# One block for eight stages: the barriers between the stages of a layer chain give way to waits on data

## The reference

```python
x = x + _L0_xattn_ref(_layernorm(x), ctx, ctx, Wq, Wk, Wv, Wo)    # 32 heads of 16, grouped keys
x = x + _L0_ffn_ref(_layernorm(x), c1_w, c2_w, w1, w2t)           # one hidden unit of each block of 32
x = x + _L1_xattn_ref(_layernorm(x), ctx, Wq, Wk, Wv, Wo)         # 16 heads of 96 over ctx and x
x = x + _L1_ffn_ref(_layernorm(x), W, b, lora_A, lora_B)          # Hadamard rotation, W, low-rank part
x = x + _L2_xattn_ref(_layernorm(x), ctx, mask, Wq, Wk, Wv, Wo, q_norm_w, k_norm_w)  # 32 heads of 128
x = x + _L2_ffn_ref(_layernorm(x), weight)                        # operands rounded to fp8 by a global scale
x = x + _L3_xattn_ref(_layernorm(x), ctx, ctx)                    # correlation by Fourier transforms, top 9 lags
x = x + _L3_ffn_ref(_layernorm(x), w1, s1, w2, s2, w3, s3)        # gated unit, weights of 4 bits
```

## Time and profile before

| | |
|---|---|
| times of 3 runs | 1519.96, 1521.7, 1523.2 us; median 1521.7 |
| span of the profiled execution | 1519.0 us (the runs take 1 to 4 us more than this span) |
| PE busy | 1394.3 us, 92% of the span |
| DVE, ACT, POOL busy | 1080.1, 762.1, 718.3 us |
| stages 0 to 7 end at | 171.5, 351.7, 651.2, 684.0, 1204.1, 1246.9, 1339.0, 1519.0 us |
| PE's pause at the seven crossings | 4.26, 6.02, 3.57, 5.16, 3.97, 4.74, 3.68 us; sum 31.4 |

### The profile page before, as it was taken

One profiled execution on the slowest core, in us unless ns is written; L12 is line 12 of the kernel. 1 busy time (PEld: TensorE's weight loads), 2 busy tenths in 40 slices (PEclk: granted clock), 3 DMA queues, 4 the chain that ended last, 5 costly groups with the idle time before them and its releaser, 6 DMA issues. The chain is left out here.

```text
span 1519.0 us, 31488 instructions
## 1 busy us (share of the span) xinstructions
PE 1394.3 (92%) x11352; PEld 830.9 (55%) x11352; DVE 1080.1 (71%) x2125; ACT 762.1 (50%) x2476; POOL 718.3 (47%) x748
## 2 busy tenths in 40 slices
PE   5798599997999999887999999999999788889998
PEld 4676244445777777444655555555555335434444
DVE  7997665645666666667989888898877779966212
ACT  4777363222434432347666666666665457655111
POOL 4888551001433434845666666665665306734000
PEclk9999799999999999999999999999999898989999
DMA  7999572215999988766775655655545401546000
GB/s 189 186 174 181 124 171 42 35 35 122 174 195 184 170 142 136 127 144 147 154 150 112 113 115 111 140 109 115 105 79 79 123 3 32 127 84 112 17 12 28
DMA packets 524570, 174.63 MB, mean 115 GB/s; under 512 B 482576, under 2 KB 507600, under 8 KB 524416
## 3 DMA queue, kind: packets, MB, share of 16 engines
q1 hardware_dynamic: 524416, 172.62, 59.0%
HBM read 53.27 MB, written 2.10 MB: 36 GB/s over the span
## 5 line engine op out<-in xcount | busy, mean ns | idle before, releaser
L1946 POOL TENSOR_TENSOR a_q_ss<-a_q_ss,half 128x4 f32<-128x4 f32 x64 | 90.1, 1408 | 167.6 <-DVE a_q_ss L1855 84.0
L67 PE MATMUL bank<-a_wq_hi,xn_pair 128*128 128x512 f16 (+1 forms) x384 | 140.8, 367 | 10.9 <-DVE a_kn L1860 5.2
L1768 ACT ACTIVATE a_probs<-a_masked,a_negmax 128x128 f32<-128x128 f32 x256 | 99.6, 390 | 101.6 <-DVE a_negmax L1826 101.6
L1285 POOL TENSOR_TENSOR a_p_hl<-a_probs,a_p_hl 128x512 f16<-128x512 f32 x64 | 74.3, 1162 | 142.3 <-DVE a_p_hl L1209 142.3
L68 PE MATMUL bank<-a_wq_lo,xn_pair 128*128 128x512 f16 (+1 forms) x384 | 140.5, 366 | 0.0
L69 PE MATMUL bank<-a_wq_hi,xn_pair 128*128 128x512 f16 (+1 forms) x384 | 140.3, 365 | 0.0
L67 PE MATMUL bank<-a_wo_hi,a_o_hi 128*128 128x512 f16 x256 | 97.8, 382 | 4.4 <-DVE x_state L1842 3.5
L68 PE MATMUL bank<-a_wo_lo,a_o_hi 128*128 128x512 f16 x256 | 97.7, 382 | 0.0
L69 PE MATMUL bank<-a_wo_hi,a_o_lo 128*128 128x512 f16 x256 | 97.5, 381 | 0.0
L1961 POOL TENSOR_TENSOR a_normal<-a_probs,a_recip 128x512 f32<-128x512 f32 x64 | 90.2, 1410 | 5.0
L716 POOL TENSOR_TENSOR a_p_hl<-a_probs,a_p_hl 128x512 f16<-128x512 f32 x64 | 78.0, 1230 | 23.6 <-DVE a_p_hl L627 16.7
(11 more groups left out here) (467 smaller groups left out, 5022.4 us busy)
## 6 DMA issues: line engine op xcount, KB each, us to landing
a_no<-in_L_xattn_Wo SPq DMA_DIRECT2D x9, 1024.0 KB, 5.7
a_nq<-in_L_xattn_Wq SPq DMA_DIRECT2D x8, 1024.0 KB, 5.8
a_n_wq<-in_L_xattn_Wq SPq DMA_DIRECT2D x4, 768.0 KB, 5.7
a_n_wo<-in_L_xattn_Wo SPq DMA_DIRECT2D x4, 768.0 KB, 6.1
a_nk<-in_L_xattn_Wk SPq DMA_DIRECT2D x9, 256.0 KB, 3.0
a_nv<-in_L_xattn_Wv SPq DMA_DIRECT2D x9, 256.0 KB, 3.1
f_v_hat<-in_L_ffn_w SPq DMA_DIRECT2D x2, 1152.0 KB, 6.2
x_state<-in_x SPq DMA_DIRECT2D x8, 256.0 KB, 5.2
```

The lines of the kernel that those rows point to most:

```text
L67: pe.matmul(out, lh, rh, start=start, stop=False)
L1285: pool.tensor_tensor(p_hl[s % PN][:, 1, t, :], probs[unit(s, t) % PROBS][:, :, :].rearrange("p h n -> p (h n)"), p_hl[s % PN][:, 0, t, :], ...
L1768: m = act.activation(probs[s % 2][:, h, :], src, ACT.Exp, bias=negmax[s % 2][:, h:h + 1], accum_out=total[s % 2][:, h:h + 1])
L1946: pool.tensor_tensor(r[:, :], r[:, :], K.half[:, 0:n], ALU.pow).then_inc(root_done.sem, 1)
```

## The change

All stages are put into one block, made once in `build`; each stage appends to the five programs of that block, so an engine goes on from its last instruction of a stage to its first of the next. `end_stage` emits nothing any more. What the barrier gave is replaced as follows.

- A bank counts as free at the start: `n_free` and `n_drained` go down by one, `wait_free` leaves out the wait of a first use, and the loops of `pe.sem_inc` are gone.
- Each engine ends a stage (but the last) with `K.leave`: a drain that raises the engine's own `left` semaphore.
- The clearing of the last stage's semaphores moves into the next stage, on POOL: `clear_last_stage` waits until all five engines have left the last stage. It stands at a step of POOL's program: stage 1 at step `NT`, stage 2 at step 4, stage 3 after the root of the last row and the bias additions, stage 4 at step 2, stage 5 after the root of the last row, stage 6 at step 3. Stage 7 clears nothing.
- SP waits at the start of stages 2 and 6 until PE has left the stage before (`K.enter(sp, "pe")`), because it loads into memory that PE read.
- Two data waits are new: in stage 3 PE waits for each piece of `f_w_lo` (`merged_lo`, raised by L1273), and in stage 6 PE's first two queries wait for DVE's rows (`first_rows`, raised by L2870).

```diff
     def n_free(self, use, turn=0):
-        return turn * self.per[self.slot[use]] + self.nth[use] + 1
+        return turn * self.per[self.slot[use]] + self.nth[use]
+
+    def wait_free(self, pe, use, turn=0):
+        if self.n_free(use, turn):
+            pe.wait_ge(self.freed(use), self.n_free(use, turn))
...
     def n_drained(self, use, turn=0):
-        return turn * self.per[self.slot[use]] + self.nth[use] + 2
+        return turn * self.per[self.slot[use]] + self.nth[use] + 1
...
-        self.in_use = []
+        self.in_use, self.of_last, self.stage = [], [], 0
+        self.left = {e: nc.alloc_semaphore(name=f"left_{e}") for e in ("sp", "pe", "act", "dve", "pool")}
...
+    def enter(self, engine, *others):
+        for e in others:
+            engine.wait_ge(self.left[e], self.stage)
+
+    def leave(self, engine, name):
+        engine.drain().then_inc(self.left[name], 1)
+
+    def clear_last_stage(self):
+        self.enter(self.nc.gpsimd, *self.left)
+        self.nc.clear_and_free_semaphores(self.of_last)
+
     def end_stage(self):
-        self.nc.clear_and_free_semaphores(self.in_use)
-        self.nc.all_engine_barrier()
-        self.in_use = []
+        self.of_last, self.in_use = self.in_use, []
+        self.stage += 1
...
-        with nc.Block() as block:
-            @block.sync
-            def _(sp):
+        @K.block.sync
+        def _(sp):
+            K.enter(sp, "pe")
...
+            K.leave(sp, "sp")
...
-            @block.tensor
-            def _(pe):
-                for banks in (s_bank, o_bank, ring, y_bank):
-                    for freed in banks.freed_sems:
-                        pe.sem_inc(freed, 1)
...
+                if f < AHEAD[1][0]:
+                    pe.wait_ge(S.first_rows.sem, S.first_rows.count(f))
...
 def build(nc, a, out):
     with ExitStack() as ctx:
         K = Kernel(nc, ctx)
+        K.block = ctx.enter_context(nc.Block())
```

More of the change, by code:

```diff
@@ L99, in take_stats @@
         return dve.bn_stats(self.stats[:, at, :], self.x[:, at, :])
-    def end_stage(self):
-        self.nc.clear_and_free_semaphores(self.in_use)
-        self.nc.all_engine_barrier()
-        self.in_use = []
[L108 to L147, removed]
-            pe.sem_inc(freed, 1)
[L149 to L171, removed]
@@ new lines, in _, with turn @@
+        @K.block.sync
+        def _(sp):
+            def turn(b, src, here):
+                sp.dma_start_transpose(K.xn_pair[:, :, :, b * P:(b + 1) * P].rearrange("p a k n -> p (a k) n"),
+                                       src[:, :, :].rearrange("p a n -> p (a n)")).then_inc(here, 16)
+            for kind in ("wk", "wq", "wv"):
+                first.load(sp, kind, 0, first.w_in[kind])
+            first.load_columns(sp)
+            sp.wait_ge(last_lo_done, 1)
+            turn(LAST, last_hl, last_in)
+            first.load(sp, "wo", 0, first.w_in["wo"])
+            for b in ahead:
+                sp.wait_ge(next_lo.sem, next_lo.count(b))
+                sp.wait_ge(y_bank.filled(b), y_bank.n_filled(b))
+                turn(b, xn_hl[b % XB], next_in[b % XB])
+            sp.wait_ge(last_in, 16)
+            K.leave(sp, "sp")
@@ new lines, in _ @@
+        @K.block.tensor
+        def _(pe):
+            for b in batches:
+                if b == LAST:
+                    pe.wait_ge(last_in, 16)
+                else:
+                    pe.wait_ge(rot.next_in[b % rot.XB], 16 * (b // rot.XB + 1))
+                y_bank.wait_free(pe, b)
+                for k in range(KT):
+                    if b == 0:
+                        pe.wait_ge(rot.merged_lo.sem, rot.merged_lo.count(k))
+                    m = pair_matmul(pe, y_bank[b][:, :], tuple(t[:, k, b * P:(b + 1) * P] for t in (K.xn_hi, K.xn_lo)),
+                                    rot.merged(k), k == 0, k == KT - 1)
+                m.then_inc(y_bank.filled(b), 1)
+            for i, use in enumerate(first.MADE):
+                first.make(pe, use, K.bank[i])
+            K.leave(pe, "pe")
@@ new lines, in _ @@
+        @K.block.scalar
+        def _(act):
+            act.wait_ge(last_xn_done, 1)
+            act.activation(last_hl[:, 0, :], last_xn[:, :], ACT.Copy).then_inc(last_hi_done, 1)
+            for t in steps:
+                for b in ready(t, 1):
+                    act.wait_ge(next_root.sem, next_root.count(b))
+                    if b >= XN:
+                        act.wait_ge(next_lo.sem, next_lo.count(b - XN))
+                        act.wait_ge(next_in[b % XB], 16 * (b // XB))
+                    act.activation(xn[b % XN][:, :], K.x[:, b, :], ACT.Identity, bias=nxt.shift[:, b:b + 1],
+                                   scale=nxt.rstd[:, b:b + 1]).then_inc(next_xn.sem, 1)
+                    act.wait_ge(next_xn.sem, next_xn.count(b))
+                    act.activation(xn_hl[b % XB][:, 0, :], xn[b % XN][:, :], ACT.Copy).then_inc(next_hi.sem, 1)
+                for use in split_at(t):
+                    first.high(act, use)
+            K.leave(act, "act")
@@ L2951, in __init__ @@
         self.tab = K.sem("x3_tab")
+        self.first_rows = Steps(K.nc.alloc_semaphore(name="x3_first_rows"), [0, 1])
     def load(self, sp):
```

4419 lines of the change are left out of this document (2137 added, 2282 removed).

## The result

The changed kernel takes 1505.16 us (median of 4 runs, 1504.09 to 1505.43) against 1520.83 us before (median of 4, 1517.4 to 1523.2). The ratio is 0.9896, with a 95% interval of 0.988 to 0.9912: 1.0% faster, 15.7 us. The profiled spans are 1503.1 us and 1519.0 us.

A forecast was written before the change was run, and what follows sets the result against it. PE was taken to bound the kernel, its 31.4 us of crossing pauses being the ceiling. The terms 0 + 2.7 + 2.9 + 2.6 + 2.0 + 2.5 + 1.1 = 13.8 us off 1521.7 gave 1508, range 1500 to 1514.5.

The forecast's parts named there:

- What bounds the kernel: PE, busy 92% of the span, ends the kernel; its seven crossing pauses, together 31.4 us, cap the direct gain.
- 0 to 1: 0: Stage 0 to 1: PE's pause goes, but ACT's split still waits for a landing, so 0 us gained.
- 1 to 2: -2.7: Stage 1 to 2: SP's loads go out sooner and the load behind a_wo_hi lands sooner, 2.7 us gained.
- 2 to 3: -2.9: Stage 2 to 3: PE goes on with a wait per piece and DVE's queue starts sooner, 2.9 us gained.
- 3 to 4: -2.6: Stage 3 to 4: block end, barrier and eleven PE increments go before ACT's squares of the keys, 2.6 us gained.
- 5 to 6: -2.5: Stage 5 to 6: PE starts just behind DVE's first row, with first_rows raised row by row, 2.5 us gained.
- 6 to 7: -1.1: Stage 6 to 7: PE still waits for the last transposing transfer's landing, so only 1.1 us gained.
- 4 to 5: -2.0: Stage 4 to 5: DVE's aggregate and PE's transpose, said to read DVE's last reduction, come sooner, 2.0 us gained.
- What is added: Seven drains per engine, POOL's clearing and two new waits cost 0; without cover, clearing up to 5 us in all.
- Rival E: POOL's clear, waiting for all five engines, blocks POOL's chain: 4 us slower at 3 us each, 1526; chance 0.05.
- The clock: After 5 to 6 and 6 to 7: nothing counted; its rival, clock stays up, adds 7.1 us, to 1501; chance 0.13.
- Rival C: Sooner loads run beside those waited for, which land no sooner: gain only 7.7 us, to 1514; chance 0.19.

The follow-up runs named there:

- loads_early: The changed kernel with stage 1's first weights loaded four steps of stage 0 sooner and stage 2's first output weights right behind its first query weights; 1495.7 us.
- kv_first: loads_early with DVE's split of the first keys' weight of stage 2 ahead of the statistics of the last four rows; 1494.78 us.
- split_sooner: The changed kernel with the weight splits of stage 3 one step of its row loop sooner; 1504.41 us.
- all_three: kv_first with the weight splits of stage 3 one step sooner; 1493.24 us.
- meet_all: The changed kernel with every engine waiting at the start of stages 1 to 7 until all five have left the stage before; 1507.65 us.
- clear_first: The changed kernel with the clearing of the last stage's semaphores at the very start of POOL's program of each stage; 1508.05 us.
- pause_6_long: The changed kernel with 38 increments of a semaphore that nobody reads ahead of PE's first matmul of stage 6; 1510.97 us.

## Why the prediction was right

The forecast was 1508 us with a range of 1500 to 1514.5; measured are 1505.16. The sum was 13.8 us, the gain 15.7. It was right as a whole and in most of its crossings, but that the number lies so near is in part luck. By the table, the crossings gave 12.3 us instead of 13.8 (1 to 2 and 2 to 3 were too large), 1.9 us were lost by the end of stage 1 and in stage 2, 0.4 won in stage 4, and the clock, which the sum left out, gave 5.1.

*What bounds the kernel* held: PE ends it, and only PE's pauses at the crossings could give. *0 to 1: 0* was right in its mechanism. PE's first matmuls came sooner (169.56 us) and the ones behind them no sooner, since ACT's split starts at 174.60, as late after SP's issue as before. What I missed is what the longer, later pause does to the clock: 13.6 us at 0.50 behind it, against 3.4 and 3.4 us in two pieces before. It cost at most 0.8 us: the offset is +0.7 us at 177.54 and +1.5 at 182.07 and still at 190.35. Of the +1.2 us up to the end of stage 1, 0.9 are already there at PE's last matmul of stage 0 (169.46 against 168.52), where nothing is changed.

*1 to 2: -2.7* measured -1.7. The step that failed is "Landing: 1.4 to 3.9 sooner; I take 2.7, the middle". Stage 1 ended 1.2 us later than before, so times are to be taken from PE's last matmul in it. From there the queries' weights go out 4.0 us sooner, and the `Wo` load, which is tied to DVE's split of the keys' weight behind DVE's additions and statistics, 1.5 us sooner (5.4 us behind PE instead of 6.9), both as I had said. But from issue to split `Wo` took 6.7 us, where it was 6.9: that the load ahead of it had been under way for longer gave next to nothing, and the term came out near its lower end. `loads_early` shows that this load was the bound and `kv_first` that DVE's queue is next.

*2 to 3: -2.9* measured -2.2. The pause went as said, 3.57 to 0.26 us, and PE ran through the rows early; but it then stood 3.08 us for the last split weight. My cap was PE's head start; the loop over DVE, ACT and POOL passed on less. `split_sooner` and `all_three` show the pause halved when the splits stand a step sooner, and `meet_all` shows how little the head start was worth: with PE held 1.5 us longer at the crossing, its queries start 27.2 us after its last matmul of stage 2 (646.60 to 673.77), against 26.9 us in the changed kernel (648.78 to 675.68).

*3 to 4: -2.6*, *5 to 6: -2.5* and *6 to 7: -1.1* were right to 0.1 us.

*4 to 5: -2.0* measured -2.1, but not by the way that I gave. PE's transpose at 1204.82 does not read what DVE's last reduction gave. It reads the first column of `big`, the largest of the weight (L2877), which DVE wrote in stage 4 (L1912). In the changed kernel PE makes it ahead of that reduction:

```profile
1195.97 0.27 PE L2712 MATMUL bank<-ident,f_big 128*1 128x128 f32 x1
...
1197.24 0.67 DVE L1768 TENSOR_REDUCE f_row_max<-xn_rows 128x1 f32<-128x512 f32 x1
1198.03 0.18 DVE L2673 BATCH_NORM_AGGREGATE f_mv<-stats 128x2 f32<-128x6 f32 x1
1198.13 0.25 DVE L2666 TENSOR_REDUCE f_one<-bank 1x1 f32<-1x128 f32 x1
```

What bounds the crossing now is DVE's queue: the aggregate comes 0.1 us behind the reduction's end instead of 1.3, and DVE's answer to PE's transpose right behind it. That the two ways give nearly the same number is luck.

*What is added* was not seen as a cost in the table, and with `clear_first`, which takes the clearing's cover away, the kernel is slower. Rival E (POOL's clear) did not come.

*The clock* is the part where I was half right. I counted nothing, gave the rival 7.1 us, and the traces show 5.1 (3.3 in stage 6, 1.8 in stage 7). Not all of that follows from the shorter pauses. Of the 3.3 us, 2.0 are there by 1271 us of the kernel before; the other 1.3 come at 1317 to 1322 us, where the kernel before is at 0.50 far from the crossing. And at 6 to 7, among the seven traces with a pause of 2.5 to 2.7 us, the clock stays at 1.00 behind it in two (the changed kernel and `kv_first`) and is at 0.50 for 2.9 to 3.3 us in five, which keep 1.1 to 1.3 of the 1.8 us. The row that I set against the rival, 0.50 behind a pause of 2.10 us, is real, and is there after the change too; but at that same matmul four of 13 traces keep 1.00, and the row says nothing of another crossing. I also read the clock at too few places. The kernel before is at 0.50 behind 0 to 1, 1 to 2 and 3 to 4 too (3.4 us each), and for 10.2 us at 4 to 5, where the changed kernel has 6.8:

```profile
1202.90:1213.10 10.20, 4.58 (x8) 2.02 (x9) 6.50 (x18) 4.49 (x7) 1.23 (x4) 0.50 0.22 71
...
1199.80:1206.50 6.70, 4.97 (x7) 2.10 (x8) 5.57 (x13) 4.80 (x8) 0.50 (x2) 0.50 0.00 0
```

That gives nothing that can be seen: the changed kernel is 7.1 us ahead at PE's second matmul of stage 5 and 7.1 at its last. The Trainium skill, "TensorE: Matmul & The Clock Gate", section "HAM oscillation", has the rule that long pauses throw the clock back; `pause_6_long` agrees, with 0.50 after 5.97 us where the same kernel has 1.00 after 2.21. The four traces of 13 that keep 1.00 after 2.10 us, and the nine that don't, are not explained by it.

*Rival C* was right about its places, the landings at 0 to 1 and 1 to 2, but not that sooner loads would hold them up: `a_n_wo` took 6.7 us from issue to split (354.24 to 360.99), as before (6.9).

What my explanation of the gain had wrong is the stress. I spoke of waits for the other engines. `meet_all` puts all of these back and costs 2.5 us, 3.6 by the ratios. The increments, 5 to 7 us with what the clock adds in stage 6, and the rest of what surrounded the barrier (the end of the block, the clearing ahead of it, the second meeting) make up the other 12 to 13. How these three share what the increments leave was not tried.

## What to carry to other kernels

Before a barrier between stages is taken out, list what runs at the crossing besides the wait itself: increments one by one on the busiest engine, clearing, the end of a block. Here those were three quarters to five sixths of the gain and could have gone with the meeting kept. Then look for the landing or the queue that is waited for next: moving two loads ahead gave 9.5 us more, but only some 5 while the barrier stood. And a pause of the matmul engine is to be priced with the clock behind it, by what traces show after pauses of about that length at that very place, and in more than one of them: here a low stretch that came or stayed away was worth up to 1.8 us, as much as a crossing.

## What the runs showed of the hardware

One semaphore increment in PE's program took 0.15 us of its time (11 of them 1.66 us, 7 of them 1.06 us), though each lasts 51 ns in the trace. The clock behind a pause is no function of its length alone. At 5 to 6 all pauses up to 3.0 us (nine traces) left it at 1.00 and all from 3.7 us on (four) went with 0.50. At another point of stage 6 the same pause of 2.1 us ahead of the same matmul brought 3.4 us at 0.50 in nine traces, among them the kernel before (1332.6 to 1336.0 us) and after (1319.2 to 1322.6 us), and nothing in four.
